# Four levels of pairwise scores taken as two joint products, with the next block's first scores ahead of the second output product

## The reference, cut to what matters

```python
q = silu(x @ wq); k = sigmoid(x @ wk); v = x @ wv; f = 1 - k
sign_f = sign(f - 0.5); theta = cumsum(sign_f) * pi     # only signs: cos is +1 or -1, sin is 0
S_t = S_{t-1} * f_t + k_t v_t^T                          # per head, 128 x 128, elementwise decay f_t over the key
o_t = (q_t / sqrt(256)) S_t
out = layernorm(o * sigmoid(x @ wg1 @ wg2)) * norm_w @ wo
x = x + ga * out; then x = x + gb * ffn(layernorm(x) modulated)
```

## Time and profile before

| | |
|---|---|
| median of 3 runs | 1872.35 us |
| the profiled execution's own time | 1875.95 us |
| its span, first to last instruction | 1874.0 us |
| TensorE matmul busy | 1838.9 us, 98% |
| VectorE busy | 1393.5 us, 74% |
| ScalarE busy | 737.2 us, 39% |
| mean granted TensorE clock | 0.995 of 2.4 GHz |
| attention | up to about 1273 us; crossing to about 1332 us; feed-forward to the end |

### The profile page before, as it was taken

The page is one execution under the profiler, slowest core; times in us unless marked ns, Lnnn a source line. Parts: engine busy times, 40 slices in busy tenths (PEclk is TensorE's granted clock), DMA queues, the critical chain, the costliest instruction groups (busy, mean ns, idle before and its releaser), DMA issues. The chain is left out here.

```text
span 1874.0 us, 56458 instructions
## 1 busy us (share of the span) xinstructions
PE 1838.9 (98%) x24873; PEld 1649.0 (88%) x24873; DVE 1393.5 (74%) x2821; ACT 737.2 (39%) x1425; POOL 377.9 (20%) x309
## 2 busy tenths in 40 slices
PE   6899999999999999999999999999999999999998
PEld 5788989999899998999989999897898898888887
DVE  5677776777777777677776777779778778778775
ACT  3333343333333334333343333443444544544543
POOL 1011001110010100111001110012244344344343
PEclk9999999999999999999999999999999999999999
DMA  7002000010000100001000010001111111111110
GB/s 281 3 9 84 25 25 25 24 47 25 25 25 24 45 27 25 24 25 48 25 25 24 25 48 25 24 28 65 68 57 57 68 57 57 68 57 56 68 57 34
DMA packets 42650, 84.88 MB, mean 45 GB/s; under 512 B 2324, under 2 KB 2856, under 8 KB 42408
## 3 DMA queue, kind: packets, MB, share of 16 engines
q1 hardware_dynamic: 41336, 79.18, 12.0%
q10 hardware_dynamic: 1072, 2.10, 0.3%
HBM read 47.72 MB, written 33.55 MB: 43 GB/s over the span
## 5 line engine op out<-in xcount | busy, mean ns | idle before, releaser
L130 POOL TENSOR_TENSOR ln_rs<-ln_ve,mhalf 128x2 f32<-128x2 f32 x64 | 71.3, 1114 | 1016.8 <-DVE ln_ve L125 1016.8
L331 POOL TENSOR_TENSOR xs<-xs,y 128x512 f32<-128x512 f32 x64 | 83.5, 1305 | 369.5 <-DVE y L711 369.5
L1103 PE MATMUL bank<-hT_hi,wq_hi 128*128 128x256 f32 x512 | 152.2, 297 | 4.5 <-DVE wq_lo L1047 4.5
L744 DVE TENSOR_TENSOR Tot<-Tot 128x256 f32<-128x256 f32 (+2 forms) x192 | 46.9, 244 | 143.2 <-PE lvl L1180 113.3
L1103 PE MATMUL bank<-hT_hi,wk_hi 128*128 128x256 f32 x512 | 151.6, 296 | 0.0
L136 DVE TENSOR_SCALAR xn<-xs,ln_mv,ln_rs 128x512 f32<-128x512 f32 x128 | 124.5, 1013 | 29.5 <-POOL ln_rs L130 29.5
L1103 PE MATMUL bank<-hT_lo,wq_hi 128*128 128x256 f32 x512 | 146.1, 285 | 0.0
L1103 PE MATMUL bank<-hT_hi,wq_lo 128*128 128x256 f32 x512 | 145.9, 285 | 0.0
L1103 PE MATMUL bank<-hT_hi,wk_lo 128*128 128x256 f32 x512 | 145.7, 285 | 0.0
L1103 PE MATMUL bank<-hT_lo,wk_hi 128*128 128x256 f32 x512 | 145.5, 284 | 0.0
L1103 PE MATMUL bank<-xk_hi,fk_hi 128*128 128x256 f32 x512 | 145.1, 283 | 0.2 <-DVE xk_lo L843 0.2
(11 more groups left out here) (180 smaller groups left out, 5708.0 us busy)
## 6 DMA issues: line engine op xcount, KB each, us to landing
xs<-in_L_attn_x SPq DMA_DIRECT2D x32, 512.0 KB, 3.6
x_scratch<-xs SPq DMA_DIRECT2D x32, 512.0 KB, 3.2
xs<-x_scratch SPq DMA_DIRECT2D x32, 512.0 KB, 3.5
out<-xs SPq DMA_DIRECT2D x31, 512.0 KB, 2.8
mod_raw<-in_L_wmod SPq DMA_DIRECT2D x6, 1024.0 KB, 13.2
raw_q<-in_L_attn_wq SPq DMA_DIRECT2D x1, 1024.0 KB, 10.3
raw_k<-in_L_attn_wk SPq DMA_DIRECT2D x1, 1024.0 KB, 13.5
raw_v<-in_L_attn_wv SPq DMA_DIRECT2D x1, 1024.0 KB, 10.0
```

What stands on the lines that cost most here:

```text
L130: pool.tensor_tensor(out=ln["rs"][:, :], in0=ln["ve"][:, :], in1=mhalf[:, :], op=ALU.pow).then_inc(ln["rstd"], 1)
L331: pool.tensor_tensor(out=dst, in0=dst, in1=y[:, ch, :], op=ALU.add).then_inc(x2_sb, 1)
L744: dve.tensor_tensor(out=Tot[:, off2:off2 + cnt2], in0=t[:, :, 0], in1=t[:, :, 1], op=ALU.mult)
L1103: last = pe.matmul(dst, lhs(a, s), rhs(b, s), start=(t == 0), stop=(t == len(terms) - 1))
```

## The change

- The levels m = 2, 4 become one pair, m = 8, 16 another. Q0, X and Q1 lie side by side in one tile QX (96 columns for each 32 rows). For a pair VectorE makes three variants of Q in X (`variants`), each of a quarter of the elements, and one `pair_product` multiplies 24 columns of Q and 24 of X with K. It has 32 products of 48 columns, like near scores, and replaces two `level_product` calls of 16 columns. `pair_merge` writes its scores into A32 with five masked copies, two of which wait for an earlier one. `pair_update` then carries Q and K over both levels with six instructions of 256 elements. The tables of decay products are formed by `first_totals`, `neighbours` and `joint`; `first_totals(n + 1)`, with 512 and 384 elements, runs in block n on VectorE, after `ln_var` and ahead of `apply_next` and `g1_low`.
- On TensorE `near_scores(n + 1)` moves from the head of block n+1 to block n, between `wo_rows(n - 1, 1)` and `output(n, 1)`. So `output(n, 1)` is directly followed by `t2(n, 0)` and `t2(n, 1)`.
- On VectorE the block begins with `first_update`, `variants`, then the diagonal; `gated_stats(n, 1)` moves from the end of block n into block n+1. `q_odd` moves behind `level_update` of m = 64. In block 30 `weight_low("k")` of quarters 0 and 1 stays around the m = 32 level.
- At the start, wq waits for the first modulation matrix to land, wk for the second, wv, wg1 and wg2 for wq, x block 1 and wo for wk, and GA and GB for wv. The matrices CB and SB are loaded in blocks 2 and 3. Their two `mod_product` calls move from block 0 to block 5, and the remaining two of block 0 move to after q pair 1 and after k pair 1. W_k and W_r of the feed-forward part are issued by SP at n = 6 in place of ScalarE at n = 2. The high half of wo is copied earlier on ScalarE in block 0.
- In the crossing the same steps are used: VectorE runs `first_update`, `variants`, `diagonal`, `first_merge`, `ogt_low` 0, `gated_stats`, `joint`, `gated_var`, `neighbours`, `ogt_low` 1, `pair_update`, `variants`, `pair_merge`, then `shift(0, "k")`, `joint`, `low(0, "k")`, `pair_update`, `pair_merge`, and so on; TensorE runs `t2`, pair product 0, wo 0, wo 1, pair product 1, four `fk_rows`, level 4, `fr_rows` 0, level 5.

```diff
+PAIRS = (2, 8)
+NL = 5
+NU = 5
+NM = 10
...
+        QX = at("QX", [P, G, QB, 96], 114)
+        Q, Qo = (QX[:, :, :, 0:32], QX[:, :, :, 64:96]), (QX[:, :, :, 32:48], QX[:, :, :, 48:64])
+        X = QX[:, :, :, 32:64]
...
+        T = {2: Tot[:, 0:512], 8: TS[:, 0:128], 32: TS[:, 256:288], 64: TS[:, 288:304], 128: TS[:, 304:312]}
+        D = {2: Tot[:, 512:1024], 8: TS[:, 128:256]}
...
                 mod_load(CA)
                 mod_load(SA)
+                sp.wait_ge(mod_in[CA], 16)
                 rows_in(w_raw["q"], env["wq"], w_in["q"])
+                sp.wait_ge(mod_in[SA], 16)
                 rows_in(w_raw["k"], env["wk"], w_in["k"])
-                sp.wait_ge(mod_cols, 1)
+                sp.wait_ge(w_in["q"], 16)
                 rows_in(w_raw["v"], env["wv"], w_in["v"])
                 rows_in(w_raw["g1"], env["wg1"], w_in["g1"])
                 rows_in(w_raw["g2"], env["wg2"], w_in["g2"])
+                sp.wait_ge(w_in["k"], 16)
                 ln_load(sp, ln, xf, 1)
                 rows_in(w_raw["o"], env["wo"], w_in["o"])
+                sp.wait_ge(w_in["v"], 16)
                 mod_load(GA)
                 mod_load(GB)
-                mod_load(CB)
-                mod_load(SB)
...
+                def first_update(n, par):
+                    dve.wait_ge(mm["lvl"], NL * n + 1)
+                    dve.wait_ge(qodd, n + 1)
+                    tq, tk = Q[par].rearrange("p g b (n two) -> p g b n two", two=2), K[par][:, :, 0::2]
+                    fq = f[:, :, :].rearrange("p g (b t) -> p g b t", b=QB)[:, :, :, 0::2]
+                    dve.tensor_tensor(out=tq[:, :, :, :, 1], in0=Qo[par], in1=fq, op=ALU.mult)
+                    dve.tensor_tensor(out=tq[:, :, :, :, 0], in0=tq[:, :, :, :, 0], in1=fq, op=ALU.mult)
+                    dve.tensor_tensor(out=tk, in0=tk, in1=f[:, :, 1::2], op=ALU.mult).then_inc(level, 1)
...
+                def neighbours(n, i):
+                    m = PAIRS[i]
+                    dve.wait_ge(tabs, 9 * n + 4 * i + 1)
+                    t, d = fours(T[m]), fours(D[m])
+                    dve.tensor_tensor(out=d[:, :, 0:3], in0=t[:, :, 0:3], in1=t[:, :, 1:4], op=ALU.mult).then_inc(tabs, 1)
+
+                def first_totals(n):
+                    dve.wait_ge(f_sb, 2 * (n + 1))
+                    dve.tensor_tensor(out=T[2].rearrange("p (g n) -> p g n", g=G), in0=f[:, :, 0::2], in1=f[:, :, 1::2], op=ALU.mult
+                                      ).then_inc(tabs, 1)
+                    neighbours(n, 0)
+
+                def variants(n, par, i):
+                    m = PAIRS[i]
+                    t, d, q, x = fours(T[m]), fours(D[m]), quarters(Q[par], m), quarters(X, m)
+                    dve.wait_ge(level, NU * n + i + 1)
+                    dve.tensor_tensor(out=x[:, :, :, 1, :], in0=q[:, :, :, 3, :], in1=spread_over(t[:, :, 2], m), op=ALU.mult)
+                    dve.tensor_tensor(out=x[:, :, :, 2, :], in0=q[:, :, :, 2, :], in1=spread_over(t[:, :, 1], m), op=ALU.mult)
+                    dve.wait_ge(tabs, 9 * n + 4 * i + 2)
+                    dve.tensor_tensor(out=x[:, :, :, 3, :], in0=q[:, :, :, 3, :], in1=spread_over(d[:, :, 1], m), op=ALU.mult
+                                      ).then_inc(x_set, 1)
+
+                def joint(n, i):
+                    m = PAIRS[i]
+                    t, d = fours(T[m]), fours(D[m])
+                    dve.wait_ge(x_set, 2 * n + i + 1)
+                    dve.tensor_tensor(out=d[:, :, 3], in0=d[:, :, 0], in1=t[:, :, 2], op=ALU.mult).then_inc(tabs, 1)
+                    dve.tensor_tensor(out=t[:, :, 1], in0=d[:, :, 1], in1=t[:, :, 3], op=ALU.mult).then_inc(tabs, 1)
+                    dve.tensor_tensor(out=T[4 * m], in0=d[:, :, 0], in1=d[:, :, 2], op=ALU.mult).then_inc(tabs, 1)
+
+                def pair_update(n, par, i):
+                    m = PAIRS[i]
+                    t, d, q, x = fours(T[m]), fours(D[m]), quarters(Q[par], m), quarters(X, m)
+                    kk = K[par][:, :, :].rearrange("p g t -> p (g t)").rearrange("p (n four m) -> p n four m", four=4, m=m)
+                    dve.wait_ge(mm["lvl"], NL * n + 2 + i)
+                    dve.wait_ge(tabs, 9 * n + 4 * i + 5)
+                    dve.tensor_tensor(out=q[:, :, :, 1, :], in0=q[:, :, :, 1, :], in1=spread_over(t[:, :, 0], m), op=ALU.mult)
+                    dve.tensor_tensor(out=q[:, :, :, 2, :], in0=q[:, :, :, 2, :], in1=spread_over(d[:, :, 0], m), op=ALU.mult)
+                    dve.tensor_tensor(out=q[:, :, :, 3, :], in0=q[:, :, :, 3, :], in1=spread_over(d[:, :, 3], m), op=ALU.mult)
+                    nb = G * P // (4 * m)
+                    for j, u in ((0, t[:, :, 1]), (1, d[:, :, 2]), (2, t[:, :, 3])):
+                        last = dve.tensor_tensor(out=kk[:, :, j, :], in0=kk[:, :, j, :], in1=u.unsqueeze(2).to_broadcast([P, nb, m]),
+                                                 op=ALU.mult)
+                    last.then_inc(level, 1)
...
+                    dve.copy_predicated(over(dst[:, :, 2, :]), grouped(far_m[:, :, 0, :]), over(sq_[:, :, 1, :])).then_inc(merged, 1)
+                    dve.copy_predicated(over(dst[:, :, 3, :]), grouped(far_m[:, :, 1, :]), over(sx[:, :, 0, :])).then_inc(merged, 1)
+                    dve.copy_predicated(over(dst[:, :, 1, :]), grouped(near_m[:, :, 0, :]), over(sq_[:, :, 0, :]))
+                    dve.wait_ge(merged, first + 2)
+                    dve.copy_predicated(A32[:, :, :].rearrange("p g (n x) -> p g n x", n=c)[:, :, :, 2 * m:4 * m],
+                                        twice[:, i, :].rearrange("p (n x) -> p n x", n=c).unsqueeze(1).to_broadcast([P, G, c, 2 * m]),
+                                        src[:, 1 - par, :, 1:3, :].rearrange("p (g n) j m -> p g n (j m)", g=G)).then_inc(merged, 1)
+                    dve.wait_ge(merged, first + 3)
+                    dve.copy_predicated(over(dst[:, :, 3, :]), grouped(near_m[:, :, 1, :]), over(sq_[:, :, 2, :])).then_inc(merged, 1)
...
                 def attention_body(n):
                     par = n % 2
+                    first_update(n, par)
+                    variants(n, par, 0)
                     diagonal(n, par)
+                    first_merge(n, par)
+                    if n > 0:
+                        gated_stats(n - 1, 1)
+                    joint(n, 0)
                     if n > 0:
                         gated_var(n - 1)
-                    for idx, m in enumerate(LEVELS, 1):
-                        level_update(n, par, m, idx)
-                        if m == 1 and n > 0:
-                            ogt_low(n - 1, 0)
-                            ogt_low(n - 1, 1)
-                        if m == 1 and n == 0:
-                            centre_wo()
-                        if m == 16 and n == 0:
-                            second_mods()
-                            spread_ready(0)
-                        if 1 < m <= 16:
-                            level_merge(n, par, m, idx)
-                        if m in (2, 4):
-                            q_silu(n + 1, 1 - par, m // 4)
-                        if m in (8, 16):
-                            dve.wait_ge(mm["t1"], 2 * (n + 2))
-                            f_signed(n + 1, 1 - par, m // 16, xn[:, 0, :])
-                        if m == 16:
-                            q_odd(n + 1, 1 - par)
-                        if m == 32:
-                            ln_stats(dve, ln, n + 2)
-                        if m == 64:
-                            ln_var(dve, ln, n + 2)
-                        if n == LAST - 1 and m in (16, 32):
-                            weight_low("k", [m // 32])
+                        ogt_low(n - 1, 0)
+                        ogt_low(n - 1, 1)
+                    else:
+                        centre_wo()
+                    neighbours(n, 1)
+                    pair_update(n, par, 0)
+                    variants(n, par, 1)
+                    pair_merge(n, par, 0)
+                    q_silu(n + 1, 1 - par, 0)
+                    joint(n, 1)
+                    q_silu(n + 1, 1 - par, 1)
+                    pair_update(n, par, 1)
+                    pair_merge(n, par, 1)
+                    if n == 0:
+                        second_mods()
+                        spread_ready(0)
+                    if n == 5:
+                        last_mods()
+                    dve.wait_ge(mm["t1"], 2 * (n + 2))
+                    f_signed(n + 1, 1 - par, 0, xn[:, 0, :])
+                    if n == LAST - 1:
+                        weight_low("k", [0])
+                    level_update(n, par, 32, 4)
+                    f_signed(n + 1, 1 - par, 1, xn[:, 0, :])
+                    if n == LAST - 1:
+                        weight_low("k", [1])
+                    ln_stats(dve, ln, n + 2)
+                    level_update(n, par, 64, 5)
+                    q_odd(n + 1, 1 - par)
+                    ln_var(dve, ln, n + 2)
+                    first_totals(n + 1)
...
```

(40 more changed lines are left out.)

212 lines of the change are left out of this document (107 added, 105 removed).

## The result

The kernel after has a median of 1852.22 us over 4 runs (1851.13 to 1852.47), the one before 1872.57 us beside it: a ratio of 0.9891 (95% interval 0.9874 to 0.9908), 20.4 us faster. The forecast was 1842 us, a gain of 30.5. The profiled execution took 1852.09 us around a span of 1850.2.

The account below looks back on a forecast made before the run. TensorE's list was taken to bound each attention block. The terms, 43.4 - 15.9 - 0.5 + 3.5 + 5 - 2 - 3 = 30.5 us gained, gave a median of 1841.8 us, range 1825 to 1862.

Parts of the forecast that it names:

- Levels in pairs: Attention blocks 0 to 30: two pair products replace four level products on TensorE, saving 1.40 us a block, 43.4 us.
- Near scores moved: Blocks 1 to 30: t2 chunk 1 waits for `gated`, a stall of 0.53 us each, 15.9 us given back.
- VectorE in time: Steady blocks: VectorE, at about 33 us, meets pair products and gate rows with 0.1 to 0.4 us spare; no stall.
- Rival 2: VectorE is late at pair products or gate rows: 1873 us, or 1857 at half of it; chance 0.14.
- Block 30: `weight_low` lengthens VectorE's chain ahead of the gate rows in block 30: 0.5 us lost.
- Start: Holding wk and wv back shortens the stop in the second modulation product: 3.5 us gained, between -3 and 7.
- rival 3: The loads in a row bring nothing at the start: about 1847 us; chance 0.07.
- Block 0: Projections between small matmuls and two modulation products fewer remove "issue" stops in block 0: 5 us gained, 0 to 8.
- Block 5: A modulation product directly before pair 1 in block 5 brings a stop: 2 us lost, 0 to 4.
- The crossing: Block 31: `dd` starts some 4 us later, the first fk rows some 2 us later; 3 us lost, -1 to 6.
- Rival 1: The stall at t2 does not come, as `gated` ends before chunk 1 is due: 1826 us; chance 0.08.
- Rival 4: Each block's new pause lowers TensorE's clock, 2.5 us a fall, 75 us in all: 1917 us; chance 0.03.

Follow-up runs that it names:

- near_back: The kernel after with near scores put back to the head of their own block, also in the crossing; 1829.51 us, ratio 0.9769.
- moved_alone: The kernel before with only near scores moved ahead of the second output product; 1893.22 us, ratio 1.0109.
- loads_held: The kernel after with wq, and all loads behind it, waiting for the second modulation product; 1849.98 us, ratio 0.9879.
- after_again: The kernel after, unchanged, profiled once more; 1851.49 us.
- mod5_apart: The kernel after with block 5's fifth modulation product moved ahead of k pair 0, away from pair product 1; 1847.72 us, ratio 0.9869.
- loads_free: The kernel after with the order of the start's loads of the kernel before; 1851.84 us, ratio 0.9890.

## Why the prediction was right, and where it was off

The mechanism, the side and the range held; the gain was two thirds of the forecast. In the order of its sum, against the traces:

- **Levels in pairs**, 1.40 a block. Measured 1.41, by near_back. A pair costs 1.01 against the 1.00 taken, the strides nothing.
- **Near scores moved**, 0.53 a block for 15.9 us. Measured 0.62 in moved_alone, 0.69 in the change, some 20.7 us for 30 blocks and 22.7 in the median. The step that failed is "They cost TensorE the same where they go", with the 0.05 us from the earlier trace rows. Behind near scores the first two matmuls of the output take 0.32 us (591.66 to 591.98), as a change of shape does, where behind the wo rows they take 0.22 (607.48 to 607.70 in the kernel before). And the transposes start 0.15 us behind VectorE's end, not 0.05. With 0.1 for each, 0.53 becomes 0.73.
- **VectorE in time.** True at all meetings, also at the gate rows, where 0.1 us was forecast and 0.06 measured. It has 31.96 us of a block and not 33: the masked copies of 64 elements cost 0.13 from start to start, where the estimate scaled from 128 elements. Rival 2 is false. On the rule that small instructions pay a fixed latency (the Trainium skill, VectorE: DVE Perf Modes, "The TRN2 errata"), the trace says as before: durations agree, 0.42 us for 256 elements, but independent instructions start 0.34 apart, and 64 elements 0.13.
- **Block 30**, 0.5. Measured 39.01 - 38.45 = 0.56.
- **Start**, 3.5. Measured 0 within the scatter of the start, which is rival 3 for this term. The step that failed is "Holding wk and wv back should shorten that". Wq is held only until the first matrix has landed: it is issued at 8.47 us and lands at 14.12, wk is issued at 11.11, so both are being moved during the stop (12.59 to 15.71). loads_held shows that the stop shrinks when neither is. The supposition that TensorE waits for its own instructions there was right.
- **Block 0**, 5. The marker came 10.75 us earlier; less one block's 1.4 for pairs and 2.2 for the two products that moved to block 5, 7.1 remain. No "issue" stop is left in block 0, where two of 2.09 and 2.21 us were, and the clock no longer falls behind them; the gate rows wait 1.65 us for `g_lo` in place of 0.91. What they had cost comes close to that: 4.3 us of stops and 1.6 for each of two falls of the clock (the price that after_again shows), less 0.7 for the longer wait of the gate rows, are 6.8, an estimate from these rows. Which of the two edits did it, the new order or the smaller number, no run shows apart.
- **Block 5**, -2 beside the 2.2 of the two products. It is 4.79 longer than a steady block, so -2.6; mod5_apart shows 2.0 of it to be the stop.
- **The crossing**, -3. Measured -4.2 by block 31, -4.0 to -4.7 by all that follows the marker of block 30 in two executions of each kernel (608.2 and 607.5 before, 612.2 twice after). The delay of `dd`, "some 4 us later", is 3.87. What was missed is that from there the whole crossing is VectorE's: it is busy for 33.4 of 35.5 us, so its longer list counts in full, not just up to the fk rows.

With the measured terms: 43.7 - 20.7 - 0.6 + 0 + 7.1 - 2.6 - 4.2 = 22.7 us, where the spans differ by 23.8. The 1.1 that remain lie mostly in blocks 1 to 3, which took 117.86 us before and take 114.29 now, 1.4 more of a gain than three steady blocks have. The profiled execution of before was 3.4 us above its median, that of after was not, so the medians differ by 20.4; the prediction carried its gain over to the median whole. The errors of the terms are not all of one sign: block 0 brought 2.1 us more than forecast, the moved scores, the start and the crossing together 9.5 less. By that luck the total is a little closer than its terms. The band of 1832 to 1856 "by the bounds of its terms" is also narrower than these bounds: added up they allow a gain between -6 and 59 us.

Rival 1 is false, the stall came in every block. Rival 4 is false as well: with a pause of 0.44 us a block the clock stays at 1.00. A fall of the clock, priced at 2.5 us, costs 1.6 where it could be compared. The swinging clock of which the Trainium skill tells (TensorE: Matmul & The Clock Gate, "A second HAM failure mode") does not appear at such a pause. The runs on the changed kernel show falls behind pauses from 1.76 to 6.30 us, and not each time: behind one of 2.21 and one of 2.08 the clock stayed up.

## What to carry to other kernels

Before an instruction group is moved, ask what it covers where it stands: the near scores were the 0.8 us in which VectorE normalised the last output, and moving them took back half of what the pairs had gained. Many small matmuls in a row want something larger between them, since with nothing but these TensorE uses up its list of instructions faster than the list arrives. And where the covered engine becomes the bound, as VectorE in the crossing, an order that serves TensorE's next step first can lose more than it wins.

## What had not been expected of the hardware

- TensorE stops with nothing named but "issue" after runs of small matmuls: after 93 of the second modulation product behind 128 of the first, 33 of a pair product behind 128, always at the same matmul. With loads under way a stop lasts 2.5 to 3.6 us at the start, without them 0.36. What it waits for is its own list of instructions, which comes by DMA. The rows of the instruction queue on the pages of before and after (packets, MB, share of 16 engines):

```profile
q8 instruction: 197, 3.23, 0.7%
q8 instruction: 165, 2.70, 0.6%
```

  Each packet has 16 KB. TensorE's matmuls and weight loads are 2 x 24873 before and 2 x 20777 after, so a packet carries some 252 of them in both kernels, and with the instructions of its sequencer 256. The stops of one execution lie whole packets apart: in the kernel before 768, 1025 and 3839 recorded instructions, which are 3, 4 and 15 times 256 within one. And in all 27 stops of 0.36 us and more in the twelve traces TensorE goes on 1.20 to 1.61 us after such a packet has landed (in the kernel after, 13.16 to 14.09 for the stop that ends at 15.71, 254.94 to 256.20 for the one that ends at 257.70). From the start of a packet to the resumption are 2.2 to 2.8 us; 128 matmuls of 2 columns with their weight loads, a packet's worth, are issued in 1.12 us (253.95 to 255.07), while projection matmuls 0.12 us apart take some 15 us for as many. What passes between the landing and the next matmul is not shown.
- Behind the same pauses, 1.66 to 1.88 and 2.37 to 2.40 us long, the clock fell in one execution and not in the next of the same kernel, at a price of 1.6 us each. The stop in block 5 did it too: 1.76 us in loads_free with a fall, 2.08 in after without.
- Between the end of an instruction on VectorE and the start of the transposes that wait for it lie 0.05 us in block 1 of before, 0.06 in block 1 of after and moved_alone, and 0.15 in each of the 30 blocks that follow in these two; why they differ stays open.
